# Moving the coming projections of three staggered attentions ahead of the output's transposes, in a 12-sublayer fp32 decoder on one core

## What is computed

```python
x = _layernorm(x + _L0_attn_ref(x, ...))          # LSTM and positional weights
x = _layernorm(x + _L0_xattn_ref(x, ctx, ctx, ..., mask))   # X0: 16 heads of 8, a mask
x = _layernorm(x + _L0_ffn_ref(x, ...))
x = _layernorm(x + _L1_attn_ref(x, ...))
x = _layernorm(x + _L1_xattn_ref(x, ctx, ctx, ...))
x = _layernorm(x + _L1_ffn_ref(x, ...))
x = _layernorm(x + _L2_attn_ref(x, ...))          # SELF2
x = _layernorm(x + _L2_xattn_ref(x, ctx, ctx, ...))         # X2: 16 heads of 8, no mask
x = _layernorm(x + _L2_ffn_ref(x, ...))
x = _layernorm(x + _L3_attn_ref(x, ...))          # MQA: rotary, one head of keys, causal
x = _layernorm(x + _L3_xattn_ref(ctx, x, ...))
x = _layernorm(x + _L3_ffn_ref(x, ...))
```

```python
q, k, v = x @ Wq + bq, c @ Wk + bk, c @ Wv + bv   # c is ctx, or x in MQA
attn = softmax(q @ k.T * scale [masked], axis=-1) # per head
out = (attn @ v, heads side by side) @ Wo + bo
```

## Time and profile before

| what | value |
|---|---|
| median of the 3 runs | 2461.74 us (2455.28 to 2464.20) |
| the profiled execution's own time | 2461.43 us |
| its span in the trace | 2458.7 us |
| PE busy / granted clock over the span | 71% / 0.819 |
| DVE, ACT, POOL busy | 56%, 39%, 24% |
| X0, its steps | 277 to 420 us |
| X2, its steps | 1239 to 1365 us |
| MQA, its steps | 1571 to 1755 us |

### The profile page before, as it was taken

The page is one execution under the profiler, slowest core; times in us unless marked ns, Lnnn a source line. Parts: engine busy times, 40 slices in busy tenths (PEclk is TensorE's granted clock), DMA queues, the critical chain, the costliest instruction groups (busy, mean ns, idle before and its releaser), DMA issues.

```text
span 2458.7 us, 45572 instructions
## 1 busy us (share of the span) xinstructions
PE 1734.5 (71%) x14699; PEld 1145.1 (47%) x14699; DVE 1365.3 (56%) x4246; ACT 956.9 (39%) x2631; POOL 584.9 (24%) x999
## 2 busy tenths in 40 slices
PE   4443698687755665797778221577799999998898
PEld 3332454354433443454455110355477777776343
DVE  2334565566677556316756777555444444444676
ACT  2223343466411232234434221232255555555343
POOL 2321322111122222101122333211133333333110
PEclk6555798699867777898989555699899999998999
DMA  5000000000000000000020000000000000000000
GB/s 189 1 1 1 1 1 0 1 0 0 1 0 0 0 0 0 0 1 1 0 89 0 1 0 0 1 1 0 1 1 0 0 0 0 0 0 1 1 0 17
DMA packets 2922, 19.05 MB, mean 8 GB/s; under 512 B 1049, under 2 KB 1177, under 8 KB 1561
## 3 DMA queue, kind: packets, MB, share of 16 engines
q1 hardware_dynamic: 2842, 18.02, 2.0%
HBM read 16.90 MB, written 1.05 MB: 7 GB/s over the span
## 4 chain that ended last, share of the span: by engine, by line
issue 40%; PE 31%; POOL 10%; DVE 7%; ACT 5%; POOLq 4%; DVEq 2%; ACTq 0%; DMA 0%; SPq 0%
POOL arena L2187 5%; PE ps L2555 5%; POOL arena L342 3%; PE ps L898 2%; PE ps L912 2%; PE ps L1434 2%; PE ps L2082 2%; PE ps L967 2%; PE ps L324 1%; PE ps L532 1%; PE ps L2093 1%; ACT tanh_c L1460 1%; ACT gates L1457 1%; PE ps L877 1%; PE ps L975 1%
## 5 line engine op out<-in xcount | busy, mean ns | idle before, releaser
L342 POOL TENSOR_TENSOR arena<-arena,C 128x1 f32<-128x1 f32 (+1 forms) x272 | 156.0, 575 | 892.5 <-DVE arena L353 590.7
L1057 DVE TENSOR_REDUCE arena<-ps 128x4 f32<-128x512 f32 x256 | 164.1, 686 | 106.2 <-PE ps L908 67.3
L433 POOL TENSOR_TENSOR arena<-arena,C 128x512 f32<-128x512 f32 x96 | 99.8, 1040 | 408.5 <-ACT arena L634 128.5
L2187 POOL TENSOR_TENSOR arena<-arena 128x512 f32<-128x512 f32 x128 | 133.4, 1043 | 248.6 <-DVE arena L2410 245.3
L1025 ACT ACTIVATE arena<-ps 128x512 f32<-128x512 f32 x256 | 132.2, 603 | 92.7 <-PE ps L924 92.7
L1434 PE MATMUL ps<-hid,WA 128*20 128x16 f32 x1024 | 57.2, 196 | 107.7 <-DVE hid L1477 107.7
L2555 PE MATMUL ps<-WA,arena 128*128 128x512 f32 x256 | 132.7, 600 | 0.4 <-ACT arena L2579 0.4
L2338 ACT ACTIVATE arena<-ps,arena 128x256 f32<-128x256 f32 x256 | 119.0, 470 | 33.1 <-DVE arena L2404 21.8
L2254 PE MATMUL ps<-arena 128*128 128x256 f32 x512 | 120.1, 386 | 0.1
L1891 PE MATMUL ps<-C,arena 128*128 128x128 f32 x32 | 13.1, 461 | 147.3 <-DVE arena L1984 107.0
L2402 DVE TENSOR_REDUCE arena<-ps 128x2 f32<-128x512 f32 x128 | 87.6, 685 | 52.1 <-PE ps L2254 51.5
(11 more groups left out here) (408 smaller groups left out, 4263.8 us busy)
## 6 DMA issues: line engine op xcount, KB each, us to landing
WA<-w_late SPq DMA_DIRECT2D x1, 4228.0 KB, 13.5
R<-rows SPq DMA_DIRECT2D x1, 2114.0 KB, 9.4
WA<-w_early SPq DMA_DIRECT2D x1, 1600.0 KB
WB<-w_rest SPq DMA_DIRECT2D x1, 1152.0 KB, 12.8
xT_all<-x_T SPq DMA_DIRECT2D x1, 1024.0 KB, 6.8
x_all<-x_tok SPq DMA_DIRECT2D x1, 1024.0 KB, 14.9
arena<-mask SPq DMA_DIRECT2D x1, 1024.0 KB
ctxT_all<-ctx_T SPq DMA_DIRECT2D x1, 1024.0 KB
```

The lines of the kernel that those rows point to most:

```text
L342: nc.gpsimd.tensor_tensor(v_(s, cols, "rstd", 0, n), v_(s, cols, "mv", 1, 2 * n - 1)[:, ::2] if n > 1 else v_(s, cols, "mv", 1, 1), cst("m ...
L1057: red = nc.vector.tensor_reduce(v_(z, ATT, "m", 4 * t, 4), heads(ps[z][t][:, :]), AXX, ALU.max)
L2187: nc.gpsimd.tensor_tensor(p, p, rec.unsqueeze(2).broadcast_to([128, 2, 256]), ALU.mult).then_inc(l_sub, 1)
```

## The change

Three things move in `satt_pe` and `satt_act`; no instruction is added or taken away, and POOL and DVE keep their lists.

- PE's transpose of the coming input (`front_x`) moves from behind the values to ahead of `fold_T`. It is written to another place, columns 128 to 255 of bank 2 of the other set, where the small product L947 has its result in columns 0 to 127.
- PE waits for ACT's copy of it (`xT_sb`) ahead of the next sequence's scores, since those write the same bank.
- PE's projections (`front_qkv`) move from behind the four output transposes to ahead of them.
- ACT's copy of the transposed input (L998) moves from behind the exponentials to ahead of them.

```diff
--- before.py
+++ after.py
@@ -853,6 +853,10 @@
             wides(0, 0, 0)
             in_turn(pool, step, finish)
 
+        def turned_x(s, d):
+
+            return ps[s][0][:, 0:128] if d == 0 else ps[(s + 1) % 2][2][:, 128:256]
+
         def satt_pe(pe, sub, kind, W, name, bias_name, mask_kind, out_w=384, out_name=None):
             out_name = out_name or name
             xt, a, st = xt_run.get(sub), att_run[sub], st_run[sub]
@@ -861,7 +865,7 @@
                 if kind == "kept":
                     return
                 pe.wait_ge(staged, nth(staged_run[sub], i, s + d))
-                nc.tensor.transpose(ps[s][0][:, 0:128], v_(s, ATT, "x"), ident).then_inc(xT_ps, 1)
+                nc.tensor.transpose(turned_x(s, d), v_(s, ATT, "x"), ident).then_inc(xT_ps, 1)
 
             def front_qkv(i, s, d):
                 if kind == "kept":
@@ -956,8 +960,12 @@
                 if before:
                     output(i, s)
                 pe.wait_ge(m_fold, nth(st, i, s))
+                if ahead:
+                    front_x(i, s, 2)
                 for t in T_ORDER:
                     fold_T(s, t).then_inc(sT_ps, 1)
+                if ahead and kind != "kept":
+                    pe.wait_ge(xT_sb, nth(xt, i, s + 2))
                 if after:
                     scores(i, s, 1)
                 va = arena[s][:, VAUG].rearrange("p (h d) -> p h d", h=HEADS)
@@ -969,14 +977,12 @@
                                               start=True, stop=True, skip_group_check=True)
                 mm.then_inc(oT_ps, 1)
                 if ahead:
-                    front_x(i, s, 2)
+                    front_qkv(i, s, 2)
                 pe.wait_ge(oT_sb, nth(a, i, s))
                 for t in range(GROUPS):
                     mm = nc.tensor.transpose(ps[s][3][:, t * 128:(t + 1) * 128],
                                              v_(s, ATT, "P", OT + 128 * t, 128), ident)
                 mm.then_inc(o_ps, 1)
-                if ahead:
-                    front_qkv(i, s, 2)
 
             def last(i, s):
                 turned(i, s)
@@ -995,7 +1001,7 @@
             def front_x(i, s, d):
                 if kind != "kept":
                     act.wait_ge(xT_ps, nth(xt, i, s + d))
-                    nc.scalar.copy(v_(s, ATT, "xcT"), ps[s][0][:, 0:128]).then_inc(xT_sb, 1)
+                    nc.scalar.copy(v_(s, ATT, "xcT"), turned_x(s, d)).then_inc(xT_sb, 1)
 
             def front_qkv(i, s, d):
                 va = arena[s][:, VAUG].rearrange("p (h d) -> p h d", h=HEADS)
```

## The result

| | before | changed |
|---|---|---|
| median of 20 runs each, us | 2456.56 | 2467.53 |
| ratio to before, 95% interval | | 1.004 (1.0033 to 1.0047) |
| span of the profiled execution, us | 2458.7 | 2468.7 |

The change makes the kernel about 10 us slower (11.0 by the medians, 10.0 by the spans). The forecast was 4.4 us less than the 2461.4 us of the profiled execution, 2457 us, in a range of 2447 to 2464 us. The result lies above the range and on the other side of the kernel before. The start of the sum was high too: 20 runs of the kernel before have a median of 2456.56 us, so the forecast is best compared as a difference, -4.4 us against +10 to +11.

A forecast was written before the change was run, and what follows sets the result against it. PE's own list was taken to bound X0 and X2, with PE waiting for POOL's spreading in MQA. Terms -9.8 - 2.8 + 0.7 + 7.5 = -4.4 us against 2461.4 gave 2457 us, range 2447 to 2464.

The forecast's parts named there:

- Behind the values: Projections directly after the values cover ACT's copy, so PE reaches L912 0.78 us earlier.
- The X0 term: X0's steps go from 8.54 to 7.84 us, bound by the maxima: -0.70 us x 14 = -9.8 us.
- The X2 term: X2's steps go from 7.45 to 7.26 us, bound by the maxima: -0.2 us x 14 = -2.8 us.
- MQA at full clock: MQA's scores start 0.83 us later, 0.78 come back behind the values: +0.05 us x 14 = +0.7 us.
- The clock in MQA: PE's standstill before the folds grows to 2.35 us; five more clock falls x 1.5 = +7.5 us.
- the one with 2468 us: Rival: copy L998 or the transpose comes late, scores start 0.5 us later in X0 and X2; 2468 us, chance 0.06.

The follow-up runs named there:

- e1: Changed kernel, with POOL's spreading of the coming queries in X0 and X2 held until DVE has cut the maxima; 2458.34 us, 1.000 of the kernel before.
- e5: e1 with PE's wait for ACT's copied transpose last of the four ahead of the scores instead of first; 2454.79 us, 0.9978 of the kernel before.
- e8: Changed kernel, with nine unused identity products on PE filling MQA's standstill before the transpose; 2457.28 us, 0.9995 of the kernel before.
- e7: Changed kernel, with DVE's first cut of the maxima written as a reduction instead of a copy; 2464.43 us, 1.0018 of the kernel before.
- e3: Changed kernel, with POOL's copy of the input ahead of its spreading of the queries in MQA; 2444.83 us, 0.9933 of the kernel before.
- e6: e5 with e3's order of POOL in MQA; 2436.38 us, 0.9904 of the kernel before.

## Why the prediction was wrong

- **Behind the values** (PE reaches L912 0.78 us earlier): right, and a little less. From the scores to the next L912 5.39 us passed in X0, and 4.67 to 4.73 now. The maxima bind at once in X2 (a wait of 0.39 us), and in X0 PE's own list and the maxima end together, as the prediction said.
- **The X0 term, -9.8 us**: wrong, it was -1.9. The step that failed is that the transposes' and projections' new places were followed on PE, ACT and DVE, but not what the earlier queries start on POOL. The earlier queries bring POOL's spreading (1.04 us) forward in X0: it began 0.4 to 0.8 us after the end of DVE's first cut, and now begins, in most steps, 0.2 to 0.3 us ahead of its start. e1 took only this meeting away and X0's 14 steps went from 117.7 to 111.4 us, -8.1 against the kernel before. The repeating steps are then 7.98 us, not the 7.84 forecast, and 0.06 us of that is a reading: the prediction took DVE's slack of 0.83 us from one step for all, but in every second one it is 0.71.
- **The X2 term, -2.8 us**: wrong, +1.4. The mechanism was right, the size of one addend was not: 0.1 us for a wait that stands ahead of three others. It took 0.2 to 0.3 us (0.31 to 0.33 against 0.05 and 0.14, e1 and e5), the step 0.22, and that ate the gain. With the wait last the step is 7.22 us, and 7.26 was forecast. The longer cast, 0.35 us, costs X2 only 0.04 us a step (e1). 1.2 us of the 14 steps' difference stem from the first step alone, whose length varied between 7.9 and 9.3 us from run to run.
- **MQA at full clock, +0.7 us**: the mechanism was right, and the wait (2.35 us) and the transpose's place (4.91 us) to 0.01 us. The same undersized addend made it +0.32 us a step instead of +0.05, 4 us over 13 steps; e5 gives 10.92.
- **The clock in MQA, +7.5 us**: that the longer standstill brings more falls was right, shown by e8. Seven falls of 1.59 us instead of four of 1.49 are +5.2 us; five more had been taken. The number was interpolated from the longest idle time alone, which the table under e8 does not bear out.
- **The rivals**: the one with 2468 us had nearly the right time, but by luck. It let ACT's copy or the transpose come late; in X0 the cut of the maxima did, and in X2 the copy came in time but its wait stood first of four. That time is also counted from 2461.4 us, not from the 2456.56 of the later runs.

The sum with measured terms: -1.9 + 1.4 + 9.6 = +9.1 us over the 42 steps; the spans differ by 10.0, the medians by 11.0. Against the forecast -4.4, X0 is 7.9 us of the miss, X2 4.2 and MQA 1.4. Where the rest of the spans' difference arose was not traced.

## What to carry to other kernels

When a producer is moved forward, follow each of its consumers to the engine on which it then runs, and look what that engine will run beside: here X0's gain was lost to an instruction of another engine that is done 2.9 us before PE needs it. Look also whether the trace of the kernel before already shows the two side by side somewhere: SELF2 did. On PE's list here, each wait behind the one that is fulfilled last cost about 0.1 us; that one should stand last. And before an instruction is moved ahead of a standstill, look where its own producer stands in its queue.

## What the runs showed of the hardware

- **DVE held by POOL.** A cast of 128x16 from and to the fast memory lasted up to 0.92 us (0.18 alone) while POOL ran a product of two fast-memory inputs, and ended within 0.03 us of POOL's end; a subtraction with two such inputs lasted 0.51 us, and up to 0.68; a reduction of the same 16 columns was not held (e7, at most 0.17 us in all 64). By the Trainium skill, "SBUF — State Buffer", section "SBUF: two separate sides", the two engines share a port pair that the first one keeps for its whole instruction, against DVE's fast copies and its operations with two inputs from there. The trace agrees in all three cases. The prediction did not use this rule.
- **Waits in a row.** On PE in MQA, 0.31 to 0.33 us passed from the end of ACT's copy to the product when its wait was the first of four (e1), and 0.05 us when it was the last (e5), both with all the others fulfilled for about 1 us or more. After POOL's spreading it was 0.22 to 0.24 us with two waits behind (e3) and 0.32 to 0.33 with three (e6). So each wait that followed took about 0.1 us.
- **The clock.** PE's clock fell in 0 to 12 of 13 steps of MQA; the table under e8 has the idle times. With the 2.35 us of idle time filled it never fell. A fall cost 1.3 to 1.6 us a step; in e1 one step was 2.7 us longer, at a granted clock of 0.75.
